# A mixture-of-experts block on one Trainium2 core: the expert counts stand later on every engine, and in another PSUM bank

## The reference

```python
h = einsum('bhid,oi,od->bho', x, weighted_sum, weight)            # token mixing
h = h + block(layernorm(h))                                       # linear attention, then an MLP
h = h + experts(layernorm(h))                                     # this case's routing

# the MLP: x + gelu(ln(x) @ w1 + b1) @ w2 + b2, and then, on all 8192 rows in order:
logits = x @ gate_w.T                        # 8 routed experts and 1 shared
rw = normalised mixer weights, up to 4 experts a row
mask = (rw > 0)
mask = mask * (cumsum(mask, axis=0) <= cap)  # the counts: how many rows before this one took it
gw = softmax(where(mask == 0, -inf, logits))
out = sum_e(w_e * y_e) + w_shared * y_shared # y = (silu(x@gate) * (x@up)) @ down
```

## Time and profile before

| what | us |
|---|---|
| median of 3 runs | 2729.38 (2725.92 to 2731.68) |
| the profiled execution, its own time | 2748.85 |
| its span | 2747.1 |
| PE busy in the span | 2405.4 (88%) |
| DVE busy | 1892.2 (69%) |
| ACT busy | 1462.3 (53%) |
| POOL busy | 1566.7 (57%) |

### The profile page before, as it was taken

One profiled execution on the slowest core, in us unless ns is written; L12 is line 12 of the kernel. 1 busy time (PEld: TensorE's weight loads), 2 busy tenths in 40 slices (PEclk: granted clock), 3 DMA queues, 4 the chain that ended last, 5 costly groups with the idle time before them and its releaser, 6 DMA issues. The chain is left out here.

```text
span 2747.1 us, 61186 instructions
## 1 busy us (share of the span) xinstructions
PE 2405.4 (88%) x22832; PEld 1738.9 (63%) x22832; DVE 1892.2 (69%) x4174; ACT 1462.3 (53%) x2731; POOL 1566.7 (57%) x1546
## 2 busy tenths in 40 slices
PE   4799999999999999999999858898888898986564
PEld 3588788888888888888887724444444444443453
DVE  2577777777777777777777736787777777865342
ACT  3466666666666666666666534434443444432232
POOL 1465656565665656565656522665566556655576
PEclk8999999999999999999999979999999999998887
DMA  4111111111121111111110020121121111100675
GB/s 146 43 61 63 41 60 61 60 44 60 60 64 40 44 40 44 36 48 36 44 40 13 10 98 24 64 72 51 47 69 67 50 41 49 36 20 9 143 137 79
DMA packets 115060, 152.21 MB, mean 55 GB/s; under 512 B 16537, under 2 KB 75917, under 8 KB 114768
## 3 DMA queue, kind: packets, MB, share of 16 engines
q1 hardware_dynamic: 88880, 124.46, 14.1%
q0 software_dynamic: 23808, 21.74, 4.5%
q10 hardware_dynamic: 2080, 2.10, 0.2%
HBM read 81.71 MB, written 90.96 MB: 63 GB/s over the span
## 5 line engine op out<-in xcount | busy, mean ns | idle before, releaser
L952 POOL TENSOR_TENSOR qkl<-fz,qkh 128x512 f16<-128x512 f32 x256 | 307.6, 1201 | 309.5 <-DVE qkh L849 305.2
L1817 POOL DMA_INDIRECT slot_dram<-xt,slot_u x256 | 257.6, 1006 | 74.6 <-issue 73.6
L521 PE MATMUL pF<-nh,qk_h 128*128 128x256 f16 x1024 | 282.0, 275 | 8.1 <-DVE nl L836 4.4
L522 PE MATMUL pF<-nh,qk_l 128*128 128x256 f16 x1024 | 281.2, 275 | 0.0
L523 PE MATMUL pF<-nl,qk_h 128*128 128x256 f16 x1024 | 281.2, 275 | 0.0
L964 POOL TENSOR_TENSOR ol<-on,oh 128x256 f16<-128x256 f32 x256 | 171.8, 671 | 153.5 <-ACT oh L786 153.5
L971 POOL TENSOR_TENSOR kvl<-kvacc,kvh 128x260 f16<-128x260 f32 x192 | 150.2, 782 | 107.8 <-ACT kvh L794 107.8
L1797 POOL TENSOR_TENSOR al<-az,ah 128x512 f16<-128x512 f32 x64 | 79.2, 1238 | 220.9 <-DVE ah L1586 220.9
L763 ACT ACTIVATE sh<-sm 128x512 f16<-128x512 f32 x256 | 159.3, 622 | 84.6 <-DVE sm L872 84.6
L846 DVE SCALAR_TENSOR_TENSOR fz<-pF,ez 128x512 f32<-128x512 f32 x256 | 175.3, 685 | 31.9 <-ACT ez L746 29.8
L740 ACT ACTIVATE rz<-pF 128x512 f32<-128x512 f32 x256 | 150.7, 589 | 86.0 <-PE pF L523 81.4
(11 more groups left out here) (313 smaller groups left out, 8577.0 us busy)
## 6 DMA issues: line engine op xcount, KB each, us to landing
xs<-in_x SPq DMA_DIRECT2D x128, 256.0 KB, 2.6
slot_dram<-blank SPq DMA_DIRECT2D x8, 1360.0 KB, 6.0
xg<-slot_dram SPq DMA_DIRECT2D x40, 272.0 KB, 3.2
h_dram<-hT SPq DMA_DIRECT2D x32, 256.0 KB, 2.1
x_dram<-x SPq DMA_DIRECT2D x32, 256.0 KB, 2.1
at_dram<-at SPq DMA_DIRECT2D x32, 256.0 KB, 2.2
x0b<-x_dram SPq DMA_DIRECT2D x16, 512.0 KB
atb<-at_dram SPq DMA_DIRECT2D x16, 512.0 KB
```

Source lines behind the costliest of these rows:

```text
L521: pe.matmul(out, wh, mh, start=first, stop=False, skip_group_check=True)
L522: pe.matmul(out, wl, mh, start=False, stop=False, skip_group_check=True)
L952: nc.gpsimd.tensor_tensor(qkl[:, pair:pair + 2, cols], fz[:, n % 2, :, :], qkh[:, pair:pair + 2, cols], ALU.subtract).then_inc(fl_ready, 1)
L1817: nc.gpsimd.indirect_dma_start(io["slot_dram"], bass.IndirectOffsetOnAxis(slot_u[:, c, k:k + 1], 0), xt[:, i % 2, c, :], None, bounds_chec ...
```

## The change

In `body` the step `counts(i-1)` moves from between the seventh and the eighth block of `w2` to behind `w2`, `var2` and `scale2`, and ahead of `gate_up`. The step moves on all engines, since all follow one order. On PE the counts go into columns 64 to 103 of the bank pL in place of columns 0 to 39 of pA[1]. The waits follow the bank: `var2` no longer waits for `cum_read`, but for `ht_ready` of two sequences before; `counts` waits for `lg_ready` (the logits have been read) in place of `ht_ready`; `mean3`, which writes all of pL, waits for `cum_read`; and a wait in `gate_up` for the last sequence goes.

```diff
                 s["w2"](i, range(7))
-                if before:
-                    s["counts"](i - 1)
                 s["w2"](i, range(7, FT))
                 if after:
                     s["var2"](i + 1)
                 if after:
                     s["scale2"](i + 1)
                 if before:
+                    s["counts"](i - 1)
                     s["gate_up"](i - 1, after, (0,))
                 s["mean3"](i, before)
...
             def var2(i):
                 if not (type(i) is int and i < 2):
-                    pe.wait_ge(cum_read, count(i, 1, -1))
+                    pe.wait_ge(ht_ready, count(i, 2, -2))
...
                 pe.wait_ge(hp_ready, count(i, DT, DT))
                 if before:
                     pe.wait_ge(lg_ready, count(i, 1, 0))
+                    pe.wait_ge(cum_read, count(i, 1, 0))
                 for t in range(DT):
                     mm = pe.matmul(pL[:, :], ones[:, :], hp[:, t, :], start=(t == 0), stop=(t == DT - 1))
...
                         pe.wait_ge(ht_ready, count(i, 2, 2))
-                        pe.wait_ge(cum_read, count(i, 1, 1))
...
             def counts(i):
                 pe.wait_ge(mask_ready, count(i, 1, 1))
-                pe.wait_ge(ht_ready, count(i, 2, 2))
+                pe.wait_ge(lg_ready, count(i, 1, 1))
                 first = True
                 for c in range(CH + 1):
-                    out = pA[1][:, c * EXPERTS:(c + 1) * EXPERTS]
+                    out = pL[:, COUNTS + c * EXPERTS:COUNTS + (c + 1) * EXPERTS]
...
-                link(lambda: V.tensor_tensor(t1[:, :, :], pA[1][:, 0:CH * E].rearrange("p (c e) -> p c e", c=CH),
+                link(lambda: V.tensor_tensor(t1[:, :, :], pL[:, COUNTS:COUNTS + CH * E].rearrange("p (c e) -> p c e", c=CH),
                                              carry[:, :].unsqueeze(1).broadcast_to([P, CH, E]), ALU.add))
-                link(lambda: V.tensor_tensor(carry[:, :], carry[:, :], pA[1][:, CH * E:(CH + 1) * E], ALU.add))
+                link(lambda: V.tensor_tensor(carry[:, :], carry[:, :], pL[:, COUNTS + CH * E:COUNTS + (CH + 1) * E], ALU.add))
...
+COUNTS = 64
```

## The result

The changed kernel is slower: 2745.68 us median of 8 runs (2737.15 to 2757.1) against 2729.41 us, ratio 1.0064 [1.0049, 1.0079]. The forecast was 2732 us, within 0.2% of no change. The change was run twice more, unchanged: 1.0037 [1.0024, 1.0051] and 1.0053 [1.0033, 1.0072]. The ratios come with their 95% interval and are not the quotients of two medians. Single executions far above the rest (2880 to 8080 us, one of e13 and two of the kernel before beside it) are left out of times and ratios.

The account below looks back on a forecast made before the run. PE, busy 88% of the span, was taken as the bound, with its wait for the mask targeted. Turn terms summed to +0.75, plus +2.0 for half speed, gave +2.7 us: median 2732, range 2722 to 2744.

Parts of the forecast that it names:

- Turn 9: E to az0 was 12.06 us with a DVE pause of 4.57; forecast 11.33, so -0.73 us.
- 11.33: Forecast length in us of E to az0 in the changed kernel, summed piece by piece; bounds 10.0 and 12.6.
- Turn 15: No var2 or added loads; mean3's 4.07 us wait for hp and its half speed relieved: -4.0 us, bounds -4.6 and +0.8.
- Turn 2: 55.53 us before, with half speed in w1 behind the transposes; forecast 54.93 without it, -0.60 us.
- E to az0: From the slot behind w2's seventh block (E) to DVE's first az (az0): about 11.15 us before; the other 43.60 untouched.
- turn 1: No wait for the mask before; E to az0 7.23 us, forecast 11.33, so +4.10 us.
- turns 3 to 8 and 10 to 14: Ordinary turns, 54.93 against 54.75 us: +1.08 and +0.90, with +2.0 for two half-speed stretches behind the transposes.
- The mask's wait and the half speed: PE's 2.76 us wait ahead of the counts and half speed behind it go; Ln starts 4.55 us earlier, spent by az0.
- 1 in 14 before: Rate of half-speed stretches in w1 behind the transposes, worth 1.0 us each; two were added, +2.0 us.
- Rival 1: Half speed often in w1 behind the transposes, 1.0 us a turn, up to 12 us: 2739 to 2744; chance 0.24.
- Rival 2: Pauses exist only under the profiler; turn 9 ordinary, turn 15 gains about 1: +3 to +6, 2736; chance 0.08.
- Rivals 4 and 6: 4: drain with loads behind Ln, 19 us, 2751 us, chance 0.03; 6: load ahead of Exp free, 2714 us, chance 0.02.

Follow-up runs that it names:

- e13: The kernel before with ten matmuls nobody reads where PE waits for the mask, ahead of the counts; 2720.06 us, ratio 0.9953.
- e9: The kernel before, unchanged, profiled again on another chip, beside e10, e11 and e12; 2726.71 us.
- e12: The changed kernel, unchanged, run again beside the kernel before on the chip of e9; 2743.0 us, ratio 1.0053.
- e3: Against the kernel before, only PE's counts and their bank move as in the change; DVE and ACT keep the old order; 2722.34 us, ratio 0.9973.
- e2: The changed kernel with the joint Ln and Exp table loaded ahead of Ln, no longer in counts; 2726.92 us, ratio 1.0007.
- e7: The changed kernel with seven matmuls nobody reads where PE waits ahead of the transposes; 2759.34 us, ratio 1.0047 to the kernel before.
- e4: The kernel of e2 with the counts step moved ahead of scale2; 2701.26 us, ratio 0.9896 to the kernel before.
- e10: The kernel of e4, unchanged, run on the chip of e9; 2709.35 us, ratio 0.9923 to the kernel before.
- e11: The kernel of e8, unchanged, run on the chip of e9; 2697.66 us, ratio 0.9892 to the kernel before.
- e8: The kernel of e4 with seven matmuls nobody reads ahead of the transposes; 2750.96 us, ratio 1.0025 to the kernel before.
- e5: The kernel before, unchanged, profiled a second time, on the chip of e6, e7 and e8; 2746.1 us.
- e6: The kernel before in its old order, with only the counts' bank and the waits of the change; 2748.11 us, ratio 1.0002.

## Why the prediction was wrong

The steps that failed are the lengths of the turns of before. In the prediction's words they are "Turn 9 ... 11.33: -0.73", "Turn 15 ... I take -4.0", "Turn 2 ... -0.60", and "a turn is 43.60 us ... and about 11.15 us from E to az0". All were read from one execution, 19.5 us above the median, with a late signal in nearly every turn. The largest part is turns 9 and 15: a gain of 4.7 us was forecast there, and the undisturbed pair e9 and e12 shows a loss of 4.5. The forecast of 11.33 for the changed kernel was right within 0.10.

Against the very trace that it started from, the forecast fails the other way. From E of turn 1 to the end of the span the first trace of before takes 1054.4 us and that of the changed kernel 1051.9, 2.5 less. In e9 before takes 1036.5, and in e12 the changed kernel 1055.4.

By steps, the forecast beside the difference of e9 and e12, one trace each from one chip (us, from az0 to az0 unless said):

| step | forecast | e12 less e9 |
|---|---|---|
| turn 1, from E to az0 | +4.10 | 11.36 - 7.84 = +3.52 |
| turn 2 | -0.60 | 55.01 - 52.75 = +2.26 |
| turns 3 to 8 and 10 to 14 | +1.08 + 0.90 + 2.0 | +3.91 + 6.15 |
| turn 9 | -0.73 | 60.16 - 56.26 = +3.90 |
| turn 15 | -4.0 | 49.96 - 49.35 = +0.61 |
| turn 16 | 0 | 42.41 - 44.11 = -1.70 |
| sum | +2.75 | +18.7 |

The rest of the 24.5 between the two spans is 5.6 ahead of E of turn 1 (4.2 of it ahead of the first xc of the stage) and 0.3 behind turn 16. The profiled execution of e12 took 9 us more than its median and that of e9 1 us; the medians differ by 16.3. The measured side exceeds the forecast by 15.9 us. Before is 19.7 shorter in e9 than in the first trace (turns 9, 15 and 16 15.2 of it, turn 2 2.8), and the changed kernel is 3.8 shorter in e12 than I had it.

- **The mask's wait and the half speed.** Their place was right, and that they go. What they were worth was not asked on the right side. e13 shows the worth of the half speed: 12 to 13 us when the clock is kept up there and the order is left alone. The wait itself was worth next to nothing, since DVE's own row goes on under it: moved away in e3, the turn is 53.12, and filled in e13, 53.18. The change removed both, and put 1.84 us of its own in their place (9.58 to 11.42): 1.29 is the load between Ln and Exp (e2), and 0.56 goes with the small instructions standing behind Exp and tn (53.74 against 53.18).
- **E to az0.** The 11.15 hid this. It is no fixed time from E, for DVE's row sets az0. At full clock it is 9.58; with half speed behind the counts it is 10.9 to 11.3 in e9, also without a late signal. In turn 9 of e9 PE comes late to E, the mask is there, and it is 6.90:

```profile
2128.27 0.38 PE L1249 MATMUL pY<-gl,w_h 128*128 128x512 f16 x1
2135.40 0.69 DVE L1580 SCALAR_TENSOR_TENSOR az<-pW,sz 128x512 f32<-128x512 f32 x1 [0.18 <-issue]
```

  The changed kernel needs 11.35 to 11.50 from E in each of the turns 1 to 14 (e12), so it cannot make up for a late E.
- **Turn 1.** As forecast in kind, and nearly in size. These are the rows of e9; E is 1689.54:

```profile
1689.32 0.38 PE L1249 MATMUL pY<-gl,w_h 128*128 128x512 f16 x1
1697.38 0.69 DVE L1580 SCALAR_TENSOR_TENSOR az<-pW,sz 128x512 f32<-128x512 f32 x1 [0.24 <-ACT sz L1462]
```

- **Turns 2 to 14.** Turn 2 of before had two stretches at half speed in the first trace and has none in e9: 52.75 in place of 55.53. The mean turn of before over turns 3 to 8 and 10 to 14 is 54.59 in e9 in place of 54.80. The changed kernel had four stretches at half speed in w1 there in e12, at 1.10 to 1.46 each, 5.3 in all, in place of two at 1.0. In the first trace of the changed kernel there were two, as forecast. "1 in 14 before" was a misreading: the first trace has such stretches in turns 9 and 15 as well.
- **Turn 9.** I set 11.33 against 12.06. Without the late signal it is 11.42 against 6.90, which is 4.52 more, less 0.60 ahead of E. Ahead of E another pause stands in both, of POOL ahead of its transfers (4.4 us in e9, 4.1 in e12), with PE waiting behind it for gz and a stretch at half speed in w1. Nothing here shows what that pause is.
- **Turn 15.** I gave the change -4.0 for relieving a pause of DVE. On a chip without late signals before has no such pause (49.35), so there is nothing to relieve. Of the 9.07 us by which turn 15 was longer in the first trace, 7.5 lie ahead of E, a part that the change leaves alone (e7, a changed kernel, has it too). Three late starts of ACT there make 4.8, and the half speed behind them 2.7:

```profile
2442.09 0.20 ACT L1477 ACTIVATE lg<-pL 128x36 f32<-128x36 f32 x1 [1.74 <-remote]
...
2444.21 0.60 ACT L1497 ACTIVATE ht<-pA 128x512 f32<-128x512 f32 x1 [1.22 <-remote]
2446.33 0.60 ACT L1497 ACTIVATE ht<-pA 128x512 f32<-128x512 f32 x1 [1.53 <-remote]
```

- **The 19.5 us by which the profiled execution exceeded the median.** The prediction set it aside ("touches mainly the pauses"). Most of it can be found against e9: turns 9, 15 and 16 are 60.12 + 58.41 + 46.43 against 56.26 + 49.35 + 44.11, 15.2 more, and the first xc of the MLP stage comes at 1611.24 in place of 1606.67, 4.6 more. So the base of my sum was an execution of another kind than the median seems to be, and -4.7 of my sum came from just those turns. That the other executions on the first chip were like e9 is not shown, for they have no trace.

The rivals. Rival 1, half speed often in w1, named the range in which the time fell, or nearly (2739 to 2744; 2740.4, 2743.0 and 2745.7 were measured). That is luck in the main. Its mechanism is a part: 2 to 5 stretches a trace, not 12. Rival 2 had the right thought, that turns 9 and 15 have nothing to give, with the wrong cause (the profiler) and a size of +3 to +6. Rivals 4 and 6: a load costs 1.28, and the one between Ln and Exp was not hidden. The case that I lacked is that before, without the disturbances of that trace, is faster by more than the change gives.

## What to carry to other kernels

Before you price a change against a turn of the trace, look for a turn that had no disturbance (waits of DVE and ACT for "issue" or "remote" were the sign here), or make one: fill a wait that lowers the clock with matmuls nobody reads, and see what the turn is then. A stretch at half speed behind a wait tells what the kernel loses to the clock, not what it gains when the wait is moved; that depends on the chain that is next, here DVE's single row. If the profiled execution stands well over the median, find the turns that hold the excess first, and take no gain from them. And where a step is moved behind a function of ACT, look at which table each function then finds: a load by hand of the joint table, with the step ahead of the scaling (e4, e10, e11), made the same move worth 0.8 to 1.1% in place of a loss of 0.4 to 0.6%. On the chip with the late signal nothing was left of that gain (e8, 1.0025).

## What the runs showed of the hardware

- Ten useless matmuls a turn, a row of 2.3 us in a wait of 2.6, made the kernel 0.47% faster (e13, 0.9953 [0.9935, 0.9972]). PE was at half speed for 17 us of the turns, where e9 had 41.
- A table load between two activations took 1.28 us, and the next activation started 1.29 behind the load's start. Taking the load away shortened the turn by 1.29 (55.03 to 53.74, e2).
- DVE's first reader of the counts starts 0.28 us behind the last row of small matmuls where DVE waits for it. In e5, e6 and e8 on one chip, and in the first trace of before, it took 1.34 us and more in nearly every turn, and up to 4.4. In e8 it was 3.5 in 12 turns, and in the same kernel on another chip the reader never waited long enough to show. On the chip of e5 to e8 before took 2746 us, on three others 2727 to 2732. What is late, and why, is open; no row of the trace shows a cause.
- Beside a stretch at half speed a late start of 1.4 us cost little: the turn was 54.6 to 55.1 with it (first trace) and 54.5 to 54.9 without (e9).
